# Graph attention: the shift is added to the scores on GpSimd instead of VectorE

## What is computed

```python
# first layer: three rounds of typed message passing, then a residual and a layer norm
for l in range(3):
    X = einsum('ne,ref->rnf', out, weights[l])
    hidden = segment_sum(X[edge_type, src] + biases[l][edge_type], dest)
    out = relu(hidden) if l + 1 < 3 else hidden
x = layernorm(x + out)
# second layer: attention over the same edges, softmax for each row node
alpha = sum(x[row] * x[col], axis=1) / (norm[row] * norm[col]) * beta
alpha = exp(alpha - segment_max(alpha, row)[row])
alpha = alpha / segment_sum(alpha, row)[row]
x = layernorm(x + segment_sum(alpha[:, None] * x[col], row))
```

## Time and profile before

| | |
|---|---|
| time, median of 3 runs | 5249.69 us (5236.56 to 5255.31) |
| span of the profiled execution | 4129.8 us |
| the profiled execution's own time | not recorded apart from its span |
| median less span | 1119.9 us |
| TensorE busy | 2926.3 us |
| VectorE busy | 2722.0 us |
| ScalarE busy | 820.3 us |
| GpSimd busy | 2587.4 us |

### The profile page before, as it was taken

How to read it: one execution, slowest core, us unless ns; L and a number is a source line. 1 busy time by engine, 2 the same in 40 slices (tenths; PEclk the granted TensorE clock), 3 DMA queues, 4 the chain that set the end, 5 groups by cost and what they waited for, 6 DMA issues and landing times.

```text
span 4129.8 us, 59123 instructions
## 1 busy us (share of the span) xinstructions
PE 2926.3 (71%) x14075; PEld 1889.2 (46%) x14077; DVE 2722.0 (66%) x9148; ACT 820.3 (20%) x1995; POOL 2587.4 (63%) x2738
## 2 busy tenths in 40 slices
PE   7899966776777677676777667776766444446998
PEld 4455544444444444444444444444444333334776
DVE  9988875666666666666666656666665333336999
ACT  2588801001100100100100010000010000003665
POOL 0677767777777770777777777437777777771000
PEclk9899988888888888888888888888887555557999
DMA  4100013322332333332233233243224111113654
GB/s 154 51 2 2 6 41 78 85 74 73 86 78 73 82 80 150 77 85 74 73 86 78 72 82 82 53 180 81 73 73 91 53 53 53 53 53 100 191 187 142
DMA packets 373888, 336.56 MB, mean 81 GB/s; under 512 B 262034, under 2 KB 326090, under 8 KB 373448
## 3 DMA queue, kind: packets, MB, share of 16 engines
q0 software_dynamic: 87104, 158.80, 15.6%
q1 hardware_dynamic: 83112, 113.25, 8.1%
q10 hardware_dynamic: 203360, 60.73, 6.1%
HBM read 225.44 MB, written 107.13 MB: 81 GB/s over the span
## 4 chain that ended last, share of the span: by engine, by line
PE 36%; DVE 34%; issue 12%; POOL 11%; ACT 4%; DMA 2%; DVEq 0%; SPq 0%; POOLq 0%; ACTq 0%
PE ps L1067 12%; POOL region L935 11%; PE ps L1012 9%; DVE region L605 9%; DVE region L539 9%; DVE region L540 7%; PE ps L1056 7%; DVE oh L534 3%; PE ps L1128 2%; PE ps L1098 2%; PE ps L1156 2%; DMA region<-x_of_type,arrays 2%; ACT ps L1214 2%; ACT region L1225 2%; DVE region L378 1%
## 5 line engine op out<-in xcount | busy, mean ns | idle before, releaser
L935 POOL DMA_INDIRECT region<-x_of_type,arrays x2418 | 2286.8, 946 | 945.6 <-issue 718.3
L1067 PE MATMUL ps<-region 128*128 128x510 f16 x4200 | 1455.6, 437 | 551.2 <-issue 297.5
L534 DVE TENSOR_SCALAR oh<-iota_w,arrays 128x102 f32<-128x102 f32 x2528 | 734.2, 292 | 1303.9 <-PE ps L1056 1265.6
L1056 PE MATMUL ps<-region,oh 128*102 x5040 | 1142.9, 332 | 552.6 <-SPq L837 357.6
L1056 PEld LDWEIGHTS ps<-region,oh 128*102 128x102 f32 x5040 | 967.8, 212 | 1129.6 <-issue 870.8
L1067 PEld LDWEIGHTS ps<-region 128*128 128x128 f16 x4200 | 443.1, 108 | 665.6 <-issue 620.3
L605 DVE TENSOR_TENSOR region<-region,ps 102x128 f32 x2520 | 713.3, 283 | 3.4 <-issue 3.1
L1225 ACT COPY region<-ps 128x510 f32<-128x510 f32 x155 | 89.8, 579 | 2374.6 <-PE ps L1067 2374.2
L539 DVE TENSOR_SCALAR region<-ps,arrays 128x640 f16<-128x640 f16 x844 | 459.3, 544 | 0.0
L918 POOL DMA_INDIRECT scattered_edges<-region x304 | 296.5, 975 | 208.1 <-DVE shiftcol L442 110.4
L540 DVE TENSOR_SCALAR region<-ps,arrays 128x510 f16<-128x510 f16 x844 | 399.5, 473 | 0.0
(11 more groups left out here) (217 smaller groups left out, 1441.7 us busy)
## 6 DMA issues: line engine op xcount, KB each, us to landing
edge_counts<-region ACTq DMA_DIRECT2D x155, 255.0 KB
region<-x_of_type,arrays POOLq DMA_INDIRECT x2418, 2.5
arrays<-edge_counts SPq DMA_DIRECT2D x40, 960.0 KB, 5.0
x_of_type<-region SPq DMA_DIRECT2D x50, 576.0 KB, 2.8
edge_absent<-region ACTq DMA_DIRECT2D x155, 127.5 KB
region<-edge_absent SPq DMA_DIRECT2D x40, 480.0 KB, 4.0
x_of_type<-x0st SPq DMA_DIRECT2D x51, 192.0 KB, 1.8
scattered_edges<-region POOLq DMA_INDIRECT x304, 2.1
```

The source lines that it names most:

```text
L534: ins = nc_.tensor_scalar(oh[:, t % U, 0:RB], iota_r, rowf[:, t % NT:t % NT + 1], None, ALU.is_equal)
L935: pool.indirect_dma_start(out=grow[:, t % GR * D:(t % GR + 1) * D], out_offset=None, in_=xt, in_offset=bass.IndirectOffsetOnAxis(ap=gix[:, ...
L1056: mm = pe.matmul(ps[0:RB, 6 + n % 2, t * D:(t + 1) * D], oh[:, u % U, 0:RB], grow[:, bass.ds(at[u % PAIRS], D)], start=True, stop=True)
L1067: mm = pe.matmul(ps[:, c, 0:CW], cl[:, q % CR, c * P:(c + 1) * P], cr[:, q % CR, :], start=False, stop=False, skip_group_check=True)
```

## The change

The adds of the shift leave VectorE's stream. They stand at the end of GpSimd's stream, behind the last gather, in the same order, on the same tiles, with the same wait for the chunk's shift (s_sh) and the same signal (s_bs). Nothing else is changed; the two remaining steps of VectorE have the same waits as before.

```diff
-            def shifted(b):
-                c, j = divmod(b, NB)
-                if j == 0:
-                    dve.wait_ge(s_sh, c + 1)
-                s_ = ring[:, b % RING, 0:SW[c]]
-                nc_.tensor_tensor(s_, s_, shift[:, c % 2, 0:SW[c]], ALU.add).then_inc(s_bs, 1)
...
-                if 0 <= i - LEAD < SK:
-                    shifted(i - LEAD)
...
+            for b in range(SK):
+                c, j = divmod(b, NB)
+                if j == 0:
+                    pool.wait_ge(s_sh, c + 1)
+                s_ = ring[:, b % RING, 0:SW[c]]
+                nc_.tensor_tensor(s_, s_, shift[:, c % 2, 0:SW[c]], ALU.add).then_inc(s_bs, 1)
```

## The result

| | before | changed |
|---|---|---|
| median | 5245.98 us (4 runs) | 5342.42 us (4 runs) |
| lowest to highest | 5236.56 to 5255.31 | 5330.98 to 5347.12 |
| ratio of the changed to before | | 1.0165, 95% interval 1.0141 to 1.0189 |

The account below looks back on a forecast made before the run. VectorE and TensorE were taken to pace the attention together. Exclusion between GpSimd and VectorE added 96.6 us (seven chunks), 16.6 (narrow chunk) and about 2 (end), +115 on 5249.7: 5364 us, range 5238 to 5425.

Parts of the forecast that it names:

- strict alternation: Attention: GpSimd's adds and VectorE's two-input steps exclude each other and take turns; +115 us, 5364 us, chance 0.40.
- TensorE is the second bound: Attention: with the adds off VectorE, TensorE paces at 1.48 us a block; gain at most 2.0 us a chunk, 0.7 taken.
- One add for one two-input step: Full attention chunk: 25 ready adds alternate with 25 of VectorE's 50 two-input steps, 34.3 us.
- A turn of 0.90 + 0.47 = 1.37 us: Attention: one GpSimd add taken at 0.90 us plus one VectorE step at 0.47, 25 times a chunk.
- The other 12.5 blocks at 1.48 us, 18.5: Rest of a full chunk: with GpSimd idle, 12.5 blocks run at TensorE's pace, 18.5 us.
- The chunk: Full attention chunk: 52.8 us for 38.97, +13.8; over chunks 0 to 6, 96.6 us.
- The narrow chunk: Last, narrow chunk, beside which chunk 7's wide adds fall: 45.1 us for 28.5, +16.6.
- The end, +2: Narrow adds of chunk 8, a quarter as long: about +2 us.
- What lies around the span: Whole program: the 1119.9 us between the traced span of 4129.8 and the median 5249.7, carried over unchanged.
- no hold-up: Rival: GpSimd's adds run beside VectorE's attention steps and TensorE paces; 5244 us, between 5234 and 5248, chance 0.32.
- one add a block: Rival: GpSimd gets in once per attention block, after two VectorE steps; chunk 46.0 us, +62, 5312 us, chance 0.20.
- the long add: Rival: each GpSimd add takes 1.5 us, with alternation; +28.8 a chunk, +239, 5488 us, chance 0.08.

Follow-up runs that it names:

- The maximum from PSUM: The changed kernel with VectorE's running maximum reading the scores from PSUM instead of the SBUF ring: 5275.99 us, ratio to before 0.9992.
- the paced kernel: The changed kernel with each GpSimd add waiting until the scores 31 tiles later are in the ring: 5322.19 us, ratio to before 1.0082.
- the three runs with unused work: The kernel before plus one GpSimd instruction a tile, result unused: adds 4285.77 us, copies 4173.30, memsets 4127.74, against 4130.66 without.
- the run with copies: The kernel before plus one GpSimd copy a tile (one operand read), result unused: 4173.30 us against 4130.66 without.

## Why the prediction was right, step by step

The likeliest case was the one that came: slower, by strict alternation, within its own range (5330 to 5425). Forecast 5364 against 5342.42, +115 us against +96.4. The attention, on which the sum rests, grew by 85.1; the 11 us between that and 96.4 no run explains, and the interval of 74 to 99 holds both. By the attention alone the time would be 5249.7 + 85.1 = 5335, still within that range but near its lower end.

- *TensorE is the second bound, so the removal is worth at most 2 us a chunk, 0.7 taken.* The maximum from PSUM, where the hold is hidden, gives 0.42 us a chunk.
- *One add for one two-input step.* Shown: 25 adds, 25 steps, in the same 31.5 us.
- *A turn of 0.90 + 0.47 = 1.37 us.* This is the term that was mis-sized: 1.27. The 0.47 is the spacing of VectorE's steps, of which by the slope of 1.04 ns a column only 0.40 is the columns' own time; that the other 0.07 overlaps the add is inferred from the sum. An add alone was guessed at 0.90; its reading comes to 1.27 - 0.40 = 0.87, and adds follow each other every 0.95 us at the start of a chunk, before VectorE's step gets in. The estimate from the Trainium skill's GPSIMD Engine Reference (section 3.1), 0.83 us before dispatch, lies 0.04 below this 0.87; the trace agrees with it within that.
- *The other 12.5 blocks at 1.48 us, 18.5.* Measured: 50.05 - 31.5 = 18.55.
- *The chunk:* 52.8 forecast, 50.05 measured; over the seven chunk lengths with wide adds beside wide scores (five equal ones, 11.1 us longer each, and two that differ somewhat) 77 us in place of 96.6.
- *The narrow chunk:* +16.6 forecast, from reduction to reduction +10.8 measured (40.37 against 29.58). The narrow maximum's turn is shorter than taken: the adds follow each other by turns after 0.96 us (beside the maximum of 90 columns, 0.09 us by the slope, and 0.87) and 1.27 (beside the weighting), 1.12 on the mean, where 1.235 was forecast.
- *The end, +2:* wrong in sign. The stage ended 2.9 us less late than the chunks add up to; why is not shown. Together 88.0 - 2.9 = 85.1 us, 1.62% of 5246.
- *What lies around the span:* wrong as to what it was, as shown, and without effect, since the sum rests on the attention, which takes the same time on both chips.

Of the rivals, no hold-up is excluded by L689 and L710; one add a block is what the paced kernel does (44.22 us, forecast 46.0 for that case), but left to itself GpSimd takes a turn after each step; the long add is excluded by its reading of 0.87 us, not 1.5.

The argument's weak place was that L534 and L423 pointed to different sides. For the steps of the attention the three runs with unused work settle it: they are held when GpSimd's instruction reads SBUF tensors, and not when it only writes. L423, with two inputs, ran beside instructions that only issue DMAs, so it said nothing against the hold. But L534 was no good witness for it either: it reads one tensor and a column of scalars, and was held beside an instruction that only issues a DMA, a case that no experiment takes up. That the prediction took its side from L534 and came out right is in part luck; what carried it was the argument that both steps and the add read two operands from SBUF. That GpSimd's reads hold them is the rule of the Trainium skill's page SBUF — State Buffer (section "Who interferes with whom"), and the runs here agree with it for VectorE's two-input steps: held by 1 and 2 operands read, not by a memset.

Open: why the stages before the attention take some 1150 us more on one chip than on the other (mean granted clock 0.76 against 0.83 of full speed), and what decides who comes next when both engines have work ready. In a full chunk of the run with copies (3931.33) the first copy was the one to wait: it lasted 1.56 us, while two VectorE steps that began beside it took 0.55 each.

## To carry to other kernels

Before an elementwise step is moved from VectorE to GpSimd, count where the operands of the VectorE steps beside it lie: here each one with two inputs in SBUF took turns with GpSimd instructions that read SBUF, and a turn cost the sum of both; a one-input copy from SBUF to SBUF was held as well. Where one of VectorE's two inputs could be read from PSUM instead, as the scores here, the two ran side by side. And read both engines' floors first: here TensorE was right behind VectorE, and with the hold hidden a chunk gained 0.42 of 38.97 us, nothing that can be measured in the program's time.

## What was not expected of the hardware

- The hold doesn't show as a wait. It lies within the instruction, 1.35 us for 0.55 on VectorE, and 1.30 for an add where undisturbed adds follow each other every 0.95; two engines at 99% in the same window was the sign.
- A GpSimd copy of one operand (128 x 384) held VectorE 0.38 us and a memset of the same size not at all; per column read the add costs 2.1 ns.
- A one-input copy of VectorE from SBUF to SBUF (L685) was held by GpSimd's adds from 0.36 to 1.15 us, while a reduction from PSUM (L695) and operations with one of two inputs in PSUM (the maximum from PSUM, 0.546 us; L736, at most 0.340) were not.
- The same kernel takes 4130.66 us on one chip and 5279.63 on another, with an attention of 338.1 us on both.
